# The sum over a head's dimensions, moved from a reduction to eight identity matmuls

## What is computed

```
x  = x + attn(cond_attention(x, cond))          # linear attention with running sums
x  = x + moe(recurrence(x, cond))               # 4 steps of the batch of 32 a tile, 8 experts, 2 taken

attn(x):  q = softmax over a head's dims of x Wq;  k = elu(x Wk) + 1;  v = x Wv
          context[d, e] = running sum of k[d] v[e] / (running sum of k[d] + eps)
          att[h, e] = sum over d of q[h, d] context[h, d, e]
          return att.reshape(.., 128) @ Wo + bo

recurrence: gates = sigmoid([x_t, h] W + b); memory = x_t Wx + bx + gate0 * (h Wh + bh)
            h = gate1 * h + (1 - gate1) * tanh(memory)
```

## Time and profile before

| | |
|---|---|
| median of 3 runs | 627.83 us (627.83 to 629.28) |
| span of the profiled execution | 625.2 us |
| VectorE (DVE) busy | 514.4 us, 82% |
| TensorE (PE) matmuls busy | 480.3 us, 77% |
| ScalarE (ACT) busy | 291.4 us, 47% |
| GpSimd (POOL) busy | 208.7 us, 33% |
| mean granted TensorE clock | 0.806 |

### The profile page before, as it was taken

The page is one execution under the profiler, slowest core; times in us unless marked ns, Lnnn a source line. Parts: engine busy times, 40 slices in busy tenths (PEclk is TensorE's granted clock), DMA queues, the critical chain, the costliest instruction groups (busy, mean ns, idle before and its releaser), DMA issues.

```text
span 625.2 us, 10470 instructions
## 1 busy us (share of the span) xinstructions
PE 480.3 (77%) x2559; PEld 362.0 (58%) x2559; DVE 514.4 (82%) x1403; ACT 291.4 (47%) x1084; POOL 208.7 (33%) x192
## 2 busy tenths in 40 slices
PE   6998467877777778877777777778877777777897
PEld 4876145556556556665655556556655655555575
DVE  4777799888988888888888988888888888988852
ACT  4554222444544455444444544455444444544465
POOL 5544433333333332222333333332222333333100
PEclk9999555677888888777777788888777777788899
DMA  5210000000000000000000000000000000000000
GB/s 158 71 35 1 0 0 2 0 5 5 6 4 3 5 4 4 4 4 4 4 4 4 4 2 2 4 4 4 4 4 4 4 4 4 4 3 3 8 6 14
DMA packets 12648, 6.44 MB, mean 10 GB/s; under 512 B 801, under 2 KB 12626, under 8 KB 12626
## 3 DMA queue, kind: packets, MB, share of 16 engines
q1 hardware_dynamic: 12626, 6.19, 3.5%
HBM read 4.09 MB, written 2.10 MB: 10 GB/s over the span
## 4 chain that ended last, share of the span: by engine, by line
PE 43%; DVE 38%; issue 12%; ACT 2%; SPq 2%; DVEq 1%; DMA 1%
PE bank L380 36%; DVE kvs L978 9%; DVE wo L1051 7%; DVE wo L1058 7%; DVE h L1066 6%; PE bank L555 4%; ACT to L768 2%; DVE gw L1023 1%; PE bank L510 1%; DVE mem L1044 1%; SPq L243 1%; DVE kv L941 1%; DMA xin<-in_x_dram 1%; PE bank L434 1%; DVE qn L970 1%
## 5 line engine op out<-in xcount | busy, mean ns | idle before, releaser
L363 POOL TENSOR_TENSOR qc<-kvs,qn 128x512 f32<-128x512 f32 x64 | 97.1, 1518 | 348.0 <-DVE qn L970 325.6
L380 PE MATMUL bank<-h,gwh 128*128 128x32 f32 x512 | 108.4, 297 | 119.1 <-DVE h L1066 118.7
L380 PEld LDWEIGHTS bank<-h,gwh 128*128 128x128 f32 x512 | 93.1, 226 | 154.2 <-DVE h L1066 152.7
L380 PE MATMUL bank<-w,h 128*128 128x512 f32 x128 | 92.2, 812 | 0.0
L766 ACT ACTIVATE th<-bank 128x32 f32<-128x32 f32 x128 | 25.5, 199 | 140.0 <-PE bank L380 139.8
L739 ACT ACTIVATE hid<-bank,gw 128x128 f32<-128x128 f32 x256 | 75.8, 365 | 30.5 <-PE bank L380 30.3
L978 DVE TENSOR_TENSOR_SCAN kvs<-scan_mask,kv 128x256 f32<-128x256 f32 x128 | 86.3, 697 | 0.0
L351 POOL TENSOR_TENSOR kv<-kv,qkv 128x512 f32<-128x512 f32 x64 | 79.4, 1260 | 10.6 <-DVE kv L941 10.6
L1066 DVE TENSOR_TENSOR_SCAN h<-tm,wo 128x64 f32<-128x64 f32 x128 | 60.6, 474 | 15.7 <-ACT tm L774 14.2
L1044 DVE TENSOR_TENSOR_SCAN mem<-th,bank 128x64 f32<-128x64 f32 x128 | 34.0, 266 | 45.2 <-PE bank L380 44.9
L380 PEld LDWEIGHTS bank<-w,hsq 128*128 128x128 f32 x512 | 65.2, 194 | 7.4 <-issue 0.5
(11 more groups left out here) (137 smaller groups left out, 820.0 us busy)
## 6 DMA issues: line engine op xcount, KB each, us to landing
xin<-in_x_dram SPq DMA_DIRECT2D x8, 256.0 KB, 2.8
out_dram<-res SPq DMA_DIRECT2D x32, 64.0 KB
w<-in_L_ffn_w_all_dram SPq DMA_DIRECT2D x2, 512.0 KB
gwx<-in_L_cond_w_W_dram SPq DMA_DIRECT2D x1, 128.0 KB
gwh<-in_L_cond_w_W_dram SPq DMA_DIRECT2D x1, 128.0 KB
mbias<-gpart SPq DMA_DIRECT2D x6, 0.2 KB, 1.7
cwk<-in_L_cond_Wk_dram SPq DMA_DIRECT2D x1, 64.0 KB
cwv<-in_L_cond_Wv_dram SPq DMA_DIRECT2D x1, 64.0 KB
```

The source lines that it names most:

```text
L363: pool.tensor_tensor(qc[:, a:b, :, :], kvs[:, a * D:b * D, :].rearrange("p (d e) h -> p d e h", d=D // 2), qn[:, p, a:b, :].unsqueeze(2).b ...
L380: return pe.matmul(dst, w, rhs, start=start, stop=True, skip_group_check=True)
```

## The change

add_dims goes, and att with it. att_T now has two halves. Each waits for one half of qc and issues four matmuls whose stationary operand is qc for one d (128 tokens by 128 pairs of e and head) and whose moving operand is the identity. All eight add into the same 128x128 region of PSUM: that is the sum over d, transposed. Its rows come out as e by head instead of head by e, so the rows of awo are loaded in this order, by eight DMAs of 16 rows instead of one of 128. The first half of att_T takes the place of the old one before step 1, the second takes project_out's place before step 2, and project_out moves behind step 2. On ScalarE att_out moves from before the gates of step 1 to behind the tanh of memory of step 1. GpSimd's weigh, which waited for add_dims to have read qc, now waits for each half of att_T.

```diff
         LATE = [
-            (cwo[:, :], cWo), ..., (aw_raw[:, 2, :], aWv), (awo[:, :], aWo),
+            (cwo[:, :], cWo), ..., (aw_raw[:, 2, :], aWv),
+            *((awo[H * e:H * e + H, :], aWo.rearrange("(h e) c -> e h c", e=D)[e]) for e in range(D)),
...
 (weigh, POOL)
                 if half == 0:
                     pool.wait_ge(qn_done, t + 1)
-                    at_least(pool, a_red, 2 * t)
+                at_least(pool, aT_ps, 2 * t - 1 + half)
...
-            def att_T(t):
-                pe.wait_ge(a_red, 2 * t + 2)
-                at_least(pe, x1_done, t)
-                at_least(pe, x1t_sb, t)
-                pe.transpose(ATT[:, 0:P], att[:, :, :].rearrange("p h e -> p (h e)"), ident[:, :]).then_inc(aT_ps, 1)
+            def att_T(t, half):
+                pe.wait_ge(qc_done, 2 * t + half + 1)
+                if half == 0:
+                    at_least(pe, x1_done, t)
+                    at_least(pe, x1t_sb, t)
+                for d in range(half * D // 2, (half + 1) * D // 2):
+                    last = mm(ATT[:, 0:P], qc[:, d, :, :].rearrange("p e h -> p (e h)"), ident[:, :], start=d == 0)
+                last.then_inc(aT_ps, 1)
...
 (iteration, PE)
                 if has(1):
-                    att_T(t + 1)
+                    att_T(t + 1, 0)
                 if has(0):
                     step(t, p, 1)
                 if has(1):
-                    project_out(t + 1)
+                    att_T(t + 1, 1)
                 if has(-2):
                     hidden_T(t - 2, 1)
                 if has(-1):
                     hidden(t - 1, q, 0)
                 if has(0):
                     step(t, p, 2)
+                if has(1):
+                    project_out(t + 1)
...
 (iteration, ScalarE)
-                if has(1):
-                    att_out(t + 1)
                 if has(0):
                     gates(t, p, 1)
                 if has(-1):
                     gate_exp(t - 1)
                 if has(0):
                     memory_tanh(t, 1)
+                if has(1):
+                    att_out(t + 1)
...
 (DVE)
-            def add_dims(t, half):
-                a, b = half * D // 2, (half + 1) * D // 2
-                if half == 0:
-                    dve.wait_ge(qc_done, 2 * t + 2)
-                    at_least(dve, aT_ps, t)
-                dve.tensor_reduce(att[:, :, a:b].rearrange("p h e -> p e h"),
-                                  qc[:, :, a:b, :].rearrange("p d e h -> p e h d"), AX.X, ALU.add).then_inc(a_red, 1)
...
                 if has(3):
                     inverses(t + 3, 1)
-                if has(2):
-                    add_dims(t + 2, 0)
-                    add_dims(t + 2, 1)
```

More of the change, by code:

```diff
@@ L134, in adaln_attention_recurrence_moe @@
         qc = sb("qc", [P, D, D, H])
-        att = sb("att", [P, H, D])
         attT = sb("attT", [P, TOK])
@@ L174, in adaln_attention_recurrence_moe @@
             sem(n) for n in ("q_max", "ex_ready", "ex_done", "k_ready", "q_sum", "k_sum"))
-        kv_done, kv_sum, d_den, d_rec, qn_done, qc_done, a_red = (
-            sem("kv_done"), sem("kv_sum"), sem("d_den"), sem("d_rec"), sem("qn_done"), sem("qc_done"), sem("a_red"))
+        kv_done, kv_sum, d_den, d_rec, qn_done, qc_done = (
+            sem("kv_done"), sem("kv_sum"), sem("d_den"), sem("d_rec"), sem("qn_done"), sem("qc_done"))
         aT_ps, aT_sb, p_ps, x1_done, xz_done, x1t_ps, x1t_sb = (
@@ L200, in adaln_attention_recurrence_moe @@
         LATE = [
-            (cwo[:, :], cWo), (aw_raw[:, 0, :], aWq), (aw_raw[:, 1, :], aWk), (aw_raw[:, 2, :], aWv), (awo[:, :], aWo),
+            (cwo[:, :], cWo), (aw_raw[:, 0, :], aWq), (aw_raw[:, 1, :], aWk), (aw_raw[:, 2, :], aWv),
+            *((awo[H * e:H * e + H, :], aWo.rearrange("(h e) c -> e h c", e=D)[e]) for e in range(D)),
             (gwx[:, :], w_W[0:C, :]), (gwh[:, :], w_W[C:2 * C, :]), (wxw[:, :], wx_W), (whw_raw[:, :], wh_W),
@@ L720, in att_out @@
             def att_out(t):
-                act.wait_ge(aT_ps, t + 1)
+                act.wait_ge(aT_ps, 2 * t + 2)
                 at_least(act, p_ps, t)
```

## The result

The changed kernel is slower. Its four runs take 645.55 us in the median (636.61 to 654.41), those of the kernel before 627.83 (626.40 to 629.28). The four spread over 18 us, six times as far as before; every ratio in this document leaves out the runs of a kernel that are more than 1.5% above its shortest one, and here it compares the two shorter ones (636.61 and 641.02) with the kernel before and is 1.018, 95% interval 1.013 to 1.023. That is a loss of some 11 us. The profiled execution is the run of 650.08 us, so its rows show about twice as much of it.

What follows compares the result with a forecast made beforehand. Neither PE nor DVE bounds alone; the path changes hands inside each iteration. Steady iterations -21.3, then +2.0, +0.9, +0.3, -1.8 and +2.7 sum to -17.2 us: 627.8 becomes 610.6 us, range 594 to 634 us.

Steps and rivals of the forecast that it cites:

- 0.8 x 16.6 + 0.2 x 14.9 = 16.26: Mean steady iteration in us: four in five with a 3.4 us slow stretch, one in five without; 17.05 before.
- tail at full clock 3.44: PE's work from step 3 to the next step 0 without any slow stretch: 3.44 us instead of 6.03.
- the third: Rival: front, steps 0 to 2, costs 1.0 instead of 0.45 us; 17.0 us an iteration, 620 to 630 us; chance 0.18.
- the thin cover of 0.35 us: Before memory of step 2: DVE's own work hides step 2's 1.6 us delay on PE, with 0.35 us left.
- Rival 4: Clock's pattern stays, fall still before step 3: 632 us (chance 0.13), or 17.5 us an iteration and 644 us (0.10).
- a sign that it is wrong: Slow stretches that still begin before step 3, or a step 2 that is late for DVE too.
- a mean granted clock above 0.81: Sign for the prediction: TensorE's mean granted clock rises above 0.81, with slow stretches of 3.4 instead of 6.8 us.
- Relieving DVE is worth nothing: Tail: add_dims' 1.86 us an iteration is hidden by PE's slow tail; worth something only if that tail gets shorter.
- The front at the full clock: Step 0 to step 2: the eight matmuls cost the path 0.45 us; memory of step 1 comes 0.15 us later.
- Once per run: Outside the steady part: last iteration but one +2.0, one before +0.9, first +0.3, run-in -1.8, awo's loads +2.7 us.
- its dear case: Awo's eight loads at the start: +7 us if each small transfer cost a whole microsecond more in a row.
- The rule on transposes: Tail: transposes don't engage the full clock, so might keep it down; iterations towards 17.5 us, +16 us in all.

Runs made afterwards that it cites:

- e1: The kernel before with add_dims taken out and nothing put in its place, PE's work unchanged: 625.55 us, ratio 0.997 to the kernel before.
- e2: The changed kernel with DVE's add_dims kept beside the eight matmuls, its result unused: 653.52 us, ratio 1.031 to the kernel before.
- e4: The kernel before with three extra 128x384 matmuls in PE's idle stretch between step 2 and step 3: 588.84 us, ratio 0.939 to the kernel before.
- e9: The changed kernel with the eight DMAs of awo issued behind the last load of x: 643.76 us, no ratio formed.
- e5: The changed kernel with both halves of att_T moved between step 2 and step 3, project_out and att copy back: 593.96 us, ratio 0.950 to the kernel before.
- e6: e5 with one extra 128x384 matmul in front of att_T: 583.20 us, ratio 0.930 to the kernel before.
- e10: e5 with awo's DMAs behind the last load of x and one extra 128x512 matmul behind att_T: 558.28 us, ratio 0.891 to the kernel before.
- e3: The changed kernel with three extra 128x384 matmuls in PE's idle stretch between step 2 and step 3: 572.22 us, ratio 0.912 to the kernel before.

## Why the prediction was wrong

It said 610.6 us and faster with a chance of 0.70; the outcome, 645.55 us, is above its upper end of 634 us.

**The step that failed** is this one: "The clock still falls, but later (591.5), and stays at 0.50 for 3.4 us instead of 6.8", and on it "0.8 x 16.6 + 0.2 x 14.9 = 16.26". One stretch near the end of the trace, where little work is left, was taken for what all would do. Of the 19 falls that begin in the 26 iterations 7 last 3.4 us, one 6.8, six 10.2 and five 13.6. So 13 iterations take 16.4 to 16.9 us and one 14.86, as priced; but six take 17.5 to 17.6 us and six 20.4 to 21.0. All twelve have a slow front, the end of a stretch of 10.2 or 13.6 us, and the mean is 17.76 us instead of 16.26. The prices of the other cases hold: a fall behind a fast front 16.6 (16.4 to 16.9), no fall 14.9 (14.86), tail at full clock 3.44 (568.04 to 571.60, 3.56 us). The share of iterations without a fall, one in five, was near as well (7 of 26), but six of the seven have a slow front and take 17.5 to 17.6 us.

**The rival that came true** is the third, "a slow stretch that reaches into the front now doubles eight matmuls more". Its mechanism was right and its size wrong: it took 1.0 us on the front and a short fall, 17.0 us an iteration. Measured are 2.7 us on a slow front, 3.4 us on a tail that is slow throughout, both in the iterations of 21 us. The place was another than it feared, too: the thin cover of 0.35 us before memory of step 2 was never used up (that scan waits for PE in no iteration); the wait is before memory of step 1, where the prediction saw 0.15 us. The trace had a warning: in the kernel before the iteration at 139.03 us begins inside a slow stretch of 10.2 us, and its front is 1.6 us longer; the prediction looked at the steady part and at the end alone.

**Rival 4**, the pattern stays, didn't come true: the iterations don't repeat at one length. But what it was to be decided by, and what the prediction named as a sign that it is wrong, did come in part: in six of the 26 iterations, those of 20.4 to 21.0 us, the clock falls 0.5 to 0.9 us before step 3. That its 644 us lie next to the measured 645.55 is luck: it came from 17.5 us in every iteration. The sign named for success, a mean granted clock above 0.81, came as well (0.832), in a kernel that got slower: it counts how long the clock is low, not which work stands there.

**Relieving DVE is worth nothing:** right for the steady part, shown by e1 and by e2. With a fast tail add_dims does bind memory of step 0 (e4), but the iteration is not longer for it.

**The front at the full clock**, 0.45 us: measured 0.29 (memory of step 3 after 11.93 us instead of 11.64), and memory of step 1 comes less than 0.1 us later instead of 0.15. The idle stretch is 2.92 us, not 2.5. POOL's weigh, for which the prediction saw no wait, waits for PE in six places, 78.7 us in all; but from memory of step 2 to that of step 3 it is 5.5 us behind a slow front and behind a fast one, so it cost the path nothing.

**Once per run.** The third load of x: +3.2 us in its issue and +2.9 in its landing, predicted 2.7, and far from the 7 us of its dear case; by the first memory scan all eight cost 4.1 (e9). The last iteration but one: 11.09 instead of 9.81 us, +1.3 against +2.0. The one before: 12.32 instead of 13.74, faster instead of 0.9 slower, since its slow stretch is gone. The first: +0.4 against +0.3. The second, with a stretch of 13.6 us: +2.5, not foreseen. The run-in's relief: 1.6 us in e1 against 1.8.

**The rule on transposes** (the Trainium skill, "TensorE: Matmul & The Clock Gate", Part 4: PE-mode transpose) was quoted for slow tails that stay slow. Slow stretches did last longer, but they hold transposes, plain matmuls and small products alike, and no run isolates the transposes; it stays open. The same page of the Trainium skill, HAM oscillation — how this bites in real kernels, advises for matmuls with few rows to restructure the loop so that PE stays warm between the waits. This kernel's waits are others, but the runs agree: 645.55 us became 572.22 with the gap filled, and 593.96 with nothing added and the same matmuls moved into the gap.

**What stays open:** why the clock's falls settle into a fixed pattern in one kernel and wander in another, and why some stretches last 13.6 us and others 3.4. The runs show that they do, not by what rule.

## What to carry to other kernels

Before moving work onto an engine that is waited for, look where in the period it idles, and put the work there: the same eight matmuls cost 2% in the one place, and in the other the kernel was 5% faster than before the change. In a kernel in which PE idles for some us in each period, cost TensorE's work at both levels of its clock, in every part of the period, and count the iterations at each level in the whole trace, the early ones too. Taking work from an engine gives nothing where it waits anyway: the wait in front of its next instruction (here 1.31 us) is a quick test, and in this kernel it had to be read against the next wait as well. A higher mean clock is no sign of a faster kernel when more work stands in the slow stretches.

## What was not expected of the hardware

The clock stayed at 0.50 for 13.62 us in which PE was busy for 13.08 (334.53 to 348.15 of the changed kernel), while other slow stretches in the same kernel end after 3.4 us. An idle stretch of only 1.42 us still had falls behind it (e5, where 17 of 26 iterations have one, and e6); with 0.57 us (e10) and 1.0 us (e3) there were none in 26 iterations. And the spread between runs of one kernel goes with the clock: 18 us for the changed kernel, whose falls wander, and 3 to 4 us for e3 and e10, whose clock is held, and for the kernel before, whose falls repeat.
